# One set of five PSUM banks for scores, row maxima and turned shifts, each taking the bank whose last user is longest past

## The chip, the cores and the metric

The program runs on one core of a Trainium2 chip. The core has a matrix engine (TensorE, PE in the views), a vector engine (VectorE, DVE), an activation engine (ScalarE, ACT), GpSimd (POOL) and SyncE (SP), which issues most of the DMAs. Results of TensorE land in PSUM, which has eight banks of 128 partitions by 512 float32. The metric is the time of one execution in device microseconds (us). The kernel before took 790.63 us (median of 3 runs, 789.76 to 791.11).

## The reference

One transformer block with post-normalization, on x of shape (2, 1024, 512), 16 heads of 32 columns, feed-forward width 2048:

```python
qkv = jnp.einsum('bsd,ed->bse', x, w_qkv) + b_qkv            # split into q, k, v of 16 heads
scores = jnp.einsum('bhqd,bhkd->bhqk', q, k) / math.sqrt(Hd) # causal mask added
attn = jax.nn.softmax(scores, axis=-1)
out = jnp.einsum('bhqk,bhkd->bhqd', attn, v)
x = layernorm(x + (out @ w_out.T + b_out))
hidden = relu(jnp.einsum('bsd,hd->bsh', x, sign(up_weight)) * up_scale)
ffn = jnp.einsum('bsh,dh->bsd', hidden, sign(down_weight)) * down_scale * output_scale
x = layernorm(x + ffn)
```

## The kernel before, in words

**Stages.** The work comes in eight steps s = 0 to 7 of attention, one for each pair of a group of four heads and a batch, and behind them four blocks of 512 tokens of the feed-forward part. Every float32 operand is split into a high and a low part, and products are made of two or three matmuls.

**What a step computes.** For its four heads it needs three kinds of TensorE results that are small and short-lived:

- *Maxima* ("max", line 953): 48 matmuls per step that compute the scores of 128 queries against up to 512 keys, from which VectorE takes the largest value per query (line 786 with the causal mask, line 790 without). They are made one step ahead: in step s those of step s + 1.
- *Shifts* ("shift", line 964): two transposes per step that turn the maxima of 16 (head, tile) columns into rows. ScalarE (line 673) and VectorE (line 800) split each into a high and a low part, and two DMAs write these rows into the operand of the scores, so that the score matmul subtracts the maximum.
- *Scores* ("score", line 990): 48 matmuls per step, keys in rows and queries in columns, 128 to 512 columns wide. ScalarE takes the exponential of each (line 688) into a ring of 14 tiles, and GpSimd sets what the causal mask forbids to 0 (line 596).

Groups of four tiles then go into the weighted sum with v ("pv", line 1020, bank ps_heads) and the row sum ("sum", line 1014, bank ps_sum); twice per step VectorE normalizes 512 queries in four pairs of instructions ("norm", lines 812 and 814) and the next half's weighted sum waits for it. Between these, projections of later steps run ("proj", line 913, bank ps_proj, evicted by ScalarE in lines 661 and 667).

**What sets the order.** `plan()` gives each instruction of the whole program a slot number from tables; the sorted list `todo` is walked by every engine, and each issues its own part in that order. Each engine runs in its own order, and semaphores are the only ties. In steps 0 to 5 the first normalization of a step stands at slot 19.7 (PAIRED_NORM) and the second at 52.05, in the next step. In s = 6 the first stands at 18.4 (ALONE_NORM), ahead of the maxima 14 and 15, whose slots are 18.68 and 19.16, while the weighted sum that follows it stands at slot 24, behind scores 20 to 24. In s = 6 and 7 the output projection of the first tokens ("attn", line 1036), the sign of the late weights ("sign", ScalarE) and the split of the heads ("split") are woven in.

**The banks.** Eight banks: ps_proj, ps_unit0 to 2, ps_score0 and 1, ps_heads, ps_sum. Maximum n of a step takes ps_unit[n % 3] and waits until maximum n - 3 has been read (semaphore s_max, `unit_max_ready`). The two shifts take ps_unit0 and ps_unit2, and maxima 33 and 2 wait for their reads (s_ml, `shift_low_ready`). Score n takes ps_score[n % 2] and waits for the exponential of score n - 2 (s_exp, `probs_ready`). In the last step, when no maxima are left, scores go round four banks (ps_score0, ps_score1, ps_proj, ps_unit2). Afterwards the output projection uses ps_unit0 and 1, the first layer of the feed-forward part ("up", line 1063) ps_proj and ps_unit2, the second layer ("down", line 1080) ps_score0, ps_score1, ps_heads and ps_sum.

## Time and profile before

| | |
|---|---|
| median of 3 runs | 790.63 us (789.76 to 791.11) |
| the profiled execution | 792.56 us, its span 790.8 us |
| mean granted TensorE clock | 0.98 |
| busy share of the span | PE 94%, DVE 57%, POOL 45%, ACT 41% |
| chain of work that ended last, by engine | PE 74%, DVE 15%, ACT 3%, DMA 3%, issue 3% |
| a step of attention, s = 0 to 5 | about 50 us (88 us to 388 us) |
| s = 6 and 7 | about 388 us to 508 us |
| feed-forward part | 508 us to the end |

A view's time of an instruction is counted from the span's start. Matmuls are pipelined and their ends are modelled: a matmul of 512 columns shows 0.40 us, and the next starts well inside that. So TensorE's pace is read from start to start. A number in brackets at a row's end is idle time that the view sees before the instruction, with what ended it. The granted clock of TensorE is given as a share of 2.4 GHz: 1.00 is 2.4 GHz and 0.50 is 1.2 GHz.

### The profile page before, as it was taken

To read this page: it belongs to the slowest core of one execution; us is meant where nothing else is said; L and a number is where in the kernel's file an instruction comes from. 1 tells how busy PE (TensorE), PEld (TensorE's weight loads), DVE (VectorE), ACT (ScalarE), POOL (GpSimd) and SP (SyncE) were. 2 spreads that over 40 slices of the span, in tenths; PEclk is the share of its full clock that TensorE was granted. 3 is DMA by queue.
4 is the path that set the end of the run, shared out by engine and by line. 5 is a ranking of instruction groups with operands and counts; after the bars stand their busy time and mean duration, and the time that the engine had idled before them with its cause. 6 is when DMAs were issued, how large, how long until landed. Compare 5 with 4: busy or idle time off the path is not lost.

```text
span 790.8 us, 11678 instructions
## 1 busy us (share of the span) xinstructions
PE 745.9 (94%) x4032; PEld 502.7 (64%) x4032; DVE 451.8 (57%) x1086; ACT 323.9 (41%) x631; POOL 356.2 (45%) x487
## 2 busy tenths in 40 slices
PE   6899999999999999999999898999999999999994
PEld 4687555654656556565544453688778787878882
DVE  4176495785867858668565562533286329433514
ACT  5211365555555555456545556523232223221210
POOL 4451466384673945739332411442344234323333
PEclk9999999999999999999989899999999999999998
DMA  6966364434545256352467240503002001000101
GB/s 226 316 176 173 96 175 123 136 96 133 169 126 143 82 148 164 105 148 81 134 200 259 95 161 8 174 27 121 14 27 97 24 15 40 15 1 0 54 1 53
DMA packets 44619, 85.71 MB, mean 108 GB/s; under 512 B 4880, under 2 KB 13584, under 8 KB 44432
## 3 DMA queue, kind: packets, MB, share of 16 engines
q1 hardware_dynamic: 35536, 79.72, 33.6%
q10 hardware_dynamic: 9024, 5.24, 2.3%
q8 instruction: 32, 0.52, 0.3%
q14 instruction: 27, 0.22, 0.1%
HBM read 55.33 MB, written 29.36 MB: 107 GB/s over the span
## 4 chain that ended last, share of the span: by engine, by line
PE 74%; DVE 15%; issue 3%; ACT 3%; DMA 3%; POOL 1%; SPq 0%; ACTq 0%; DVEq 0%; POOLq 0%
PE ps_heads L1020 9%; PE ps_unit L953 8%; PE ps_score L990 7%; PE ps_proj L913 7%; PE ps_proj L1063 7%; PE ps_score L1080 6%; PE ps_unit L1036 6%; PE ps_sum L1014 5%; PE ps_unit L1063 5%; DVE maxes L790 4%; DVE heads_sb L812 4%; PE ps_heads L1080 3%; PE ps_sum L1080 3%; PE ps_sum L933 1%; PE ps_score L933 1%
## 5 line engine op out<-in xcount | busy, mean ns | idle before, releaser
L688 ACT ACTIVATE probs<-ps_score 128x512 f32<-128x512 f32 (+3 forms) x360 | 171.7, 492 | 173.7 <-PE ps_score L990 166.5
L632 POOL TENSOR_TENSOR hid_low<-hid_raw,hid_high 128x512 fp32r<-128x512 f32 x64 | 85.1, 1330 | 174.5 <-DVE hid_high L863 171.4
L786 DVE CUSTOM_DVE_ANT_0 ps_unit<-ps_unit,causal 128x128 f32<-128x128 f32 (+3 forms) x256 | 122.0, 511 | 67.9 <-PE ps_unit L953 66.4
L953 PE MATMUL ps_unit<-stack 96*128 96x512 f32 (+3 forms) x384 | 136.6, 371 | 9.9 <-DVE maxes L786 4.7
L990 PE MATMUL ps_score<-stack 98*128 98x512 f32 (+2 forms) x360 | 136.7, 386 | 4.1 <-ACT probs L688 2.3
L596 POOL TENSOR_SCALAR_AFFINE_SELECT probs<-probs 128x128 f32<-128x128 f32 x256 | 74.3, 297 | 139.5 <-ACT probs L688 134.8
L953 PEld LDWEIGHTS ps_unit<-stack 96*128 96x128 f32 x384 | 72.2, 191 | 57.7 <-DVE maxes L790 23.4
L863 DVE CAST hid_high<-hid_raw 128x512 fp32r<-128x512 f32 x64 | 27.1, 425 | 126.6 <-ACT hid_raw L743 126.3
L990 PEld LDWEIGHTS ps_score<-stack 98*128 98x128 f32 x360 | 68.4, 191 | 46.4 <-ACT probs L688 32.1
L790 DVE TENSOR_REDUCE maxes<-ps_unit 128x1 f32<-128x512 f32 x128 | 79.3, 685 | 21.3 <-PE ps_unit L953 21.2
L1020 PE MATMUL ps_heads<-probs,v_rows 128*32 128x512 f32 (+3 forms) x768 | 82.6, 508 | 5.9 <-DVE heads_sb L814 5.9
L812 DVE RECIPROCAL heads_sb<-ps_sum 128x128 f32<-128x128 f32 x64 | 60.8, 950 | 13.7 <-PE ps_sum L1014 13.7
L590 POOL TENSOR_TENSOR parts<-qk_full,parts 128x512 fp32r<-128x512 f32 x32 | 41.1, 1284 | 59.5 <-ACT parts L667 59.5
L609 POOL TENSOR_TENSOR added<-added,probs 128x512 f32<-128x512 f32 x48 | 60.9, 1284 | 0.0
L743 ACT ACTIVATE hid_raw<-ps_proj,up_scale 128x512 f32<-128x512 f32 x32 | 22.0, 689 | 93.0 <-PE ps_proj L1063 93.0
L1014 PE MATMUL ps_sum<-probs,ones 128*32 128x512 f32 (+3 forms) x576 | 58.0, 469 | 0.0
L913 PE MATMUL ps_proj<-x_high,w_high 128*128 128x512 f32 x116 | 45.9, 421 | 6.6 <-ACT x_high L645 6.6
L1080 PE MATMUL ps_score<-down_sb,hid_high 128*128 128x512 f32 x124 | 50.1, 404 | 0.0
L1080 PE MATMUL ps_score<-down_sb,hid_low 128*128 128x512 f32 x124 | 48.9, 395 | 0.0
L913 PE MATMUL ps_proj<-x_high,w_low 128*128 128x512 f32 x116 | 45.3, 412 | 0.0
L913 PE MATMUL ps_proj<-x_low,w_high 128*128 128x512 f32 x116 | 44.6, 404 | 0.0
L1020 PEld LDWEIGHTS ps_heads<-probs,v_rows 128*32 128x32 f32 x768 | 19.4, 111 | 39.6 <-issue 25.7
(185 smaller groups left out, 1224.4 us busy)
## 6 DMA issues: line engine op xcount, KB each, us to landing
stack<-qk_parts SPq DMA_DIRECT2D x96, 256.0 KB, 4.7
qk_parts<-parts SPq DMA_DIRECT2D x32, 512.0 KB, 2.9
v_all<-h_even ACTq DMA_DIRECT2D x16, 256.0 KB, 3.5
v_rows<-v_all SPq DMA_DIRECT2D x8, 512.0 KB, 4.2
heads_t<-heads_sb SPq DMA_DIRECT2D x16, 256.0 KB, 3.2
raw<-up_w SPq DMA_DIRECT2D x8, 512.0 KB, 3.6
x_tile<-x_rows SPq DMA_DIRECT2D x16, 256.0 KB, 4.7
raw<-down_w SPq DMA_DIRECT2D x8, 512.0 KB, 3.7
```

Source lines behind the costliest of these rows:

```text
L632: nc.gpsimd.tensor_tensor(hid[1][:, (HM * s + n) % 3, :], hid_raw[:, n % 2, :], hid[0][:, (HM * s + n) % 3, :].bitcast(FP32), ALU.subtract ...
L688: nc.scalar.activation(probs[:, (NP * s + n) % RING, 0:width], score_bank(s, n)[:, off:off + width], ACT.Exp, scale=SCALE).then_inc(s_exp, 1)
L786: nc.vector.tensor_tensor_reduce(ps_unit[n % 3][:, 0:width], ps_unit[n % 3][:, 0:width], causal[:, HALF - width:], 1.0, NEG, ALU.add, ALU.max,
L790: nc.vector.tensor_reduce(maxes[:, 1, col:col + 1], ps_unit[n % 3][:, :], AXIS_X, ALU.max).then_inc(s_max, 1)
L812: nc.vector.reciprocal(heads_sb[:, cols], ps_sum[:, cols]).then_inc(s_rc, 1)
L913: mm = nc.tensor.matmul(proj_bank(s, k)[:, :], ws[wp][:, c, t, :], xs[xp][:, c, t0:t0 + HALF], start=(m == 0), stop=(m == 11))
L953: nc.tensor.matmul(ps_unit[n % 3][:, 0:width], stack[s % 2][0:96, 1, f, h, i % 4 * P:(i % 4 + 1) * P], stack[s % 2][0:96, 0, c, h, 0:width ...
L990: nc.tensor.matmul(score_bank(s, n)[:, 0:width + off], stack[s % 2][0:98, 0, j // 4, h, j % 4 * P:(j % 4 + 1) * P], stack[s % 2][0:98, 1, ...
L1014: nc.tensor.matmul(ps_sum[rows, at:at + width], ones[:, :], tile, **args).then_inc(s_pv, 1)
L1020: mm = nc.tensor.matmul(ps_heads[rows, at:at + width], v_rows[:, s % 2, j, rows], tile, **args)
L1063: mm = nc.tensor.matmul(ps_up[n % 2][:, :], up_sb[n // 8][:, n % 8, m % DC, :], turned[s % 2][m // DC][:, m % DC, :], start=(m == 0), stop ...
L1080: mm = nc.tensor.matmul(ps_down[i][:, :], hid[part][:, (HM * s + n) % 3, i * P:(i + 1) * P], down_sb[:, down_at(n), :], start=(n == 0 and ...
```

## The change

A new function `share(todo)` walks the order once, before anything is issued, and hands out banks. It keeps the six banks ps_unit0 to 2 (0 to 2), ps_score0 and 1 (3 and 4) and ps_proj (5) in a list, in the order of their last use, the longest past first. Each score, maximum and shift takes the first bank of the list that it may use, and this bank goes to the list's end. Scores, maxima and shifts may use banks 0 to 4; the maxima and shifts of s = 0 only 0 to 2, since the early projections and the values of v use the score banks then; scores of the last step 2 to 5. `users` holds for each its bank and the user before it, and `had` the last user of each bank. TensorE now waits for the read of that user, whichever kind it was (`bank_read`), in place of the fixed waits. Shift 0 waits for the 16 maxima that it turns, where it waited for 31.

The end changes with it. The output projection's first matmul no longer waits for the last shift's read but for the last user of bank 0, maximum 47 of s = 7. The first two up matmuls wait for the last users of bank 5 and bank 2, score 47 and score 45 of s = 7; before, the first waited for score 46 and the second for score 47. The last users of the banks are: 0 maximum 47, 1 score 46 of s = 6, 2 score 45, 3 score 46, 4 score 44, 5 score 47.

```diff
+def share(todo):
+    order, had, users = [3, 4, 5, 0, 1, 2], {}, {}
+    for what, s, n in todo:
+        if what not in ("score", "max", "shift"):
+            continue
+        if what == "score":
+            may = (2, 3, 4, 5) if s == STEPS - 1 else (0, 1, 2, 3, 4)
+        else:
+            may = (0, 1, 2, 3, 4) if s else (0, 1, 2)
+        bank = next(k for k in order if k in may)
+        users[what, s, n] = bank, had.get(bank)
+        had[bank] = what, s, n
+        order.remove(bank)
+        order.append(bank)
+    return users, had
...
-        ps_turn = [ps_unit[0], ps_unit[2]]
...
-        def score_bank(s, n):
-            return (ps_score + [ps_proj, ps_unit[2]])[n % 4] if s == STEPS - 1 else ps_score[n % 2]
+        def bank(what, s, n):
+            return (ps_unit + ps_score + [ps_proj])[users[what, s, n][0]]
...
+            def bank_read(user):
+                if user is None:
+                    return
+                what, s, n = user
+                if what == "score":
+                    pe.wait_ge(s_exp, NP * s + n + 1)
+                if what == "max":
+                    pe.wait_ge(s_max, NU * s + n + 1)
+                if what == "shift":
+                    pe.wait_ge(s_ml, 2 * s + n + 1)
...
-                    if n == 2:
-                        wait(pe, s_ml, 2 * s)
-                    if n == NU1:
-                        pe.wait_ge(s_ml, 2 * s + 1)
-                    wait(pe, s_max, NU * s + n - 2)
+                    bank_read(users[what, s, n][1])
...
-                        pe.wait_ge(s_max, NU * s + NU1 - 2)
+                        pe.wait_ge(s_max, NU * s + NU0)
...
-                    if s == STEPS - 1 and n == 2:
+                    if s == STEPS - 1 and users[what, s, n][0] == 5:
                         pe.wait_ge(s_qk, NB * STEPS)
-                    if s == STEPS - 1 and n == 3:
-                        pe.wait_ge(s_ml, 2 * STEPS)
-                    if s < STEPS - 1 or n < 2:
-                        wait(pe, s_exp, NP * s + n - 1)
-                    elif n > 3:
-                        pe.wait_ge(s_exp, NP * s + n - 3)
+                    bank_read(users[what, s, n][1])
...
-                            pe.wait_ge(s_ml, 2 * STEPS)
                             pe.wait_ge(s_sign, 2)
                             pe.wait_ge(s_wol, 2)
+                    if s == 0 and m == 0 and i < 2:
+                        bank_read(last_user[i])
...
-                        if s == 0:
-                            pe.wait_ge(s_exp, NP * STEPS - 1)
-                    if s == 0 and n == 1:
-                        pe.wait_ge(s_exp, NP * STEPS)
+                    if s == 0 and n < 2:
+                        bank_read(last_user[(5, 2)[n]])
```

No instruction changes its place on any engine. What changes is the bank in a row and the semaphore that it waits for. The first place is TensorE in s = 3, scores 21 to 26 and maximum 16 of the next step, with projections between them. Before:

```order
L990 MATMUL ps_score1<-stack1 128x512 [waits probs_ready]
L913 MATMUL ps_proj<-x_high,w_high 128x512
L990 MATMUL ps_score0<-stack1 128x512 [waits probs_ready]
L913 MATMUL ps_proj<-x_high,w_high 128x512
L990 MATMUL ps_score1<-stack1 128x512 [waits probs_ready]
L990 MATMUL ps_score0<-stack1 128x512 [waits probs_ready]
L913 MATMUL ps_proj<-x_high,w_high 128x512
L990 MATMUL ps_score1<-stack1 128x512 [waits probs_ready]
L913 MATMUL ps_proj<-x_low,w_high 128x512
L990 MATMUL ps_score0<-stack1 128x512 [waits probs_ready]
L953 MATMUL ps_unit1<-stack0 128x512 [waits unit_max_ready,stack_filled_q1]
```

and with the change (lines 990, 953 and 913 are 1013, 981 and 945 there):

```order
L1013 MATMUL ps_unit1<-stack1 128x512 [waits unit_max_ready]
L945 MATMUL ps_proj<-x_high,w_high 128x512
L1013 MATMUL ps_unit2<-stack1 128x512 [waits unit_max_ready]
L945 MATMUL ps_proj<-x_high,w_high 128x512
L1013 MATMUL ps_unit0<-stack1 128x512 [waits probs_ready]
L1013 MATMUL ps_score0<-stack1 128x512 [waits unit_max_ready]
L945 MATMUL ps_proj<-x_high,w_high 128x512
L1013 MATMUL ps_score1<-stack1 128x512 [waits probs_ready]
L945 MATMUL ps_proj<-x_low,w_high 128x512
L1013 MATMUL ps_unit1<-stack1 128x512 [waits probs_ready]
L981 MATMUL ps_unit2<-stack0 128x512 [waits probs_ready,stack_filled_q1]
```

Nothing has moved. Scores that waited for an exponential two scores back now wait for a maximum or an exponential five users back.

The second place is TensorE in s = 6, from maximum 14 of the next step over scores 19 to 24 to the weighted sum that waits for the first normalization. Before:

```order
L953 MATMUL ps_unit2<-stack1 128x384 [waits unit_max_ready]
L990 MATMUL ps_score1<-stack0 128x512 [waits probs_ready]
L953 MATMUL ps_unit0<-stack1 128x512 [waits unit_max_ready]
L990 MATMUL ps_score0<-stack0 128x512 [waits probs_ready]
L990 MATMUL ps_score1<-stack0 128x512 [waits probs_ready]
L990 MATMUL ps_score0<-stack0 128x512 [waits probs_ready]
L990 MATMUL ps_score1<-stack0 128x512 [waits probs_ready]
L990 MATMUL ps_score0<-stack0 128x512 [waits probs_ready]
L1020 MATMUL ps_heads<-probs,v_rows 32x512 [waits probs_ready,heads_normalized]
L1020 MATMUL ps_heads<-probs,v_rows 32x512 [waits probs_ready] x3
```

and with the change (1020 is 1043 and so on):

```order
L981 MATMUL ps_unit1<-stack1 128x384 [waits probs_ready]
L1013 MATMUL ps_unit2<-stack0 128x512 [waits unit_max_ready]
L981 MATMUL ps_unit0<-stack1 128x512 [waits unit_max_ready]
L1013 MATMUL ps_score0<-stack0 128x512 [waits probs_ready]
L1013 MATMUL ps_score1<-stack0 128x512 [waits unit_max_ready]
L1013 MATMUL ps_unit1<-stack0 128x512 [waits unit_max_ready]
L1013 MATMUL ps_unit2<-stack0 128x512 [waits probs_ready]
L1013 MATMUL ps_unit0<-stack0 128x512 [waits unit_max_ready]
L1043 MATMUL ps_heads<-probs,v_rows 32x512 [waits probs_ready,heads_normalized]
L1043 MATMUL ps_heads<-probs,v_rows 32x512 [waits probs_ready] x3
```

Nothing has moved here either. Score 22 (the first with ps_unit1) now waits for the read of maximum 14, the first row, and score 24 for that of maximum 15, the third; VectorE reads both behind the normalization that the last two rows wait for.

## Rows read from the trace of the kernel before

**Rows 1.** The page, busy time of each engine over the whole span

```profile
PE 745.9 (94%) x4032; PEld 502.7 (64%) x4032; DVE 451.8 (57%) x1086; ACT 323.9 (41%) x631; POOL 356.2 (45%) x487
```

**Rows 2.** TensorE's waits, whole span: what waited, for what: us in total, times, longest

```profile
PE ps_heads L1020 <- DVE heads_sb L814: 5.9, 8, 1.4
...
PE ps_score L990 <- ACT probs L688: 2.3, 11, 0.3
...
PE ps_unit L953 <- DVE shift_l L800: 1.9, 8, 0.6
```

**Rows 3.** TensorE's timeline, s = 3: start, us, instruction, [idle before it]

```profile
255.43 0.50 PE L990 MATMUL ps_score<-stack 98*128 98x512 f32 x1
...
256.01 0.40 PE L990 MATMUL ps_score<-stack 98*128 98x512 f32 x1
256.24 0.40 PE L913 MATMUL ps_proj<-x_high,w_high 128*128 128x512 f32 x1
...
261.07 0.64 PE L1020 MATMUL ps_heads<-probs,v_rows 128*32 128x512 f32 x4
```

**Rows 4.** VectorE's timeline, the same stretch and the maxima behind it

```profile
260.21 0.29 DVE L814 TENSOR_TENSOR heads_sb<-ps_heads,heads_sb 128x128 f32<-128x128 f32 x1
...
263.46 7.87 DVE L790 TENSOR_REDUCE maxes<-ps_unit 128x1 f32<-128x512 f32 x13 [1.17 <-PE ps_unit L953]
```

**Rows 5.** TensorE's timeline, behind shift 0, in s = 3 and s = 6

```profile
273.17 0.34 PE L990 MATMUL ps_score<-stack 98*128 98x384 f32 x1
273.66 0.39 PE L953 MATMUL ps_unit<-stack 96*128 96x256 f32 x1 [0.15 <-DVE shift_l L800]
...
432.81 0.39 PE L953 MATMUL ps_unit<-stack 96*128 96x256 f32 x1 [0.63 <-DVE shift_l L800]
```

**Rows 6.** TensorE's timeline, the end of s = 3

```profile
285.01 0.51 PE L990 MATMUL ps_score<-stack 98*128 98x256 f32 x2
...
287.42 0.27 PE L964 MATMUL ps_unit<-ident,row_max 128*16 128x128 f32 x1
```

**Rows 7.** TensorE's timeline, third score of s = 0

```profile
88.61 0.50 PE L990 MATMUL ps_score<-stack 98*128 98x512 f32 x1 [0.28 <-ACT probs L688]
```

**Rows 8.** Stretches: from:to, length, each engine's busy us, clock, DMA share, GB/s

```profile
284.00:287.40 3.40, 3.02 (x12) 1.78 (x12) 2.36 (x11) 2.36 (x7) 1.45 (x5) 1.00 0.47 160
383.70:387.10 3.40, 2.70 (x10) 1.31 (x9) 2.57 (x11) 2.33 (x6) 1.45 (x5) 1.00 0.50 178
387.10:390.50 3.40, 3.40 (x35) 1.73 (x34) 0.39 (x2) 0.91 (x3) 0.59 (x2) 0.50 0.89 204
411.00:414.40 3.40, 2.27 (x12) 0.59 (x16) 2.23 (x6) 1.28 (x2) 2.36 (x1) 0.50 0.19 63
```

**Rows 9.** TensorE's timeline, weighted and row sums behind s = 5, then a score

```profile
387.45 1.08 PE L1020 MATMUL ps_heads<-probs,v_rows 128*32 128x256 f32 x8
...
390.17 0.58 PE L990 MATMUL ps_score<-stack 98*128 98x384 f32 x1
```

**Rows 10.** TensorE's timeline, first matmul of the output projection

```profile
447.99 0.77 PE L1036 MATMUL ps_unit<-w_out_high,t_even_high 128*128 128x512 f32 x1 [0.85 <-DVE shift_l L800]
```

**Rows 11.** VectorE's timeline, s = 6: maxima 14 and 15 of s = 7 are stored

```profile
412.47 0.14 DVE L786 DVE_READ_ACCUMULATOR2_ANT maxes<- 128x1 f32 x1
...
413.12 0.14 DVE L786 DVE_READ_ACCUMULATOR2_ANT maxes<- 128x1 f32 x1
```

**Rows 12.** TensorE's timeline, s = 6: scores 20 and 21, then the weighted sum

```profile
408.04 0.99 PE L990 MATMUL ps_score<-stack 98*128 98x512 f32 x2 [0.22 <-ACT probs L688]
...
412.13 1.08 PE L1020 MATMUL ps_heads<-probs,v_rows 128*32 128x512 f32 x4 [1.22 <-DVE heads_sb L814]
```

**Rows 13.** Timeline of TensorE and ScalarE, start of the feed-forward part

```profile
498.70 1.10 PE L1063 MATMUL ps_proj<-t_even_high,up_a 128*128 128x512 f32 x4
498.90 0.28 ACT L688 ACTIVATE probs<-ps_unit 128x128 f32<-128x128 f32 x1 [0.37 <-PE ps_unit L990]
...
506.79 0.50 PE L1080 MATMUL ps_heads<-down_sb,hid_high 128*128 128x512 f32 x1 [0.70 <-DVE heads_sb L814]
```

More of the change, by code:

```diff
@@ L426, in build @@
         todo = plan()
+        users, last_user = share(todo)
         block = top.enter_context(nc.Block())
@@ L672, in _ @@
                     act.wait_ge(s_mt, 2 * s + n + 1)
-                    nc.scalar.activation(shift_h[:, :], ps_turn[n][0:NU0, 0:P], ACT.Copy,
+                    nc.scalar.activation(shift_h[:, :], bank(what, s, n)[0:NU0, 0:P], ACT.Copy,
                                          scale=-1.0).then_inc(s_mh, 1)
@@ L789, in _ @@
                     else:
-                        nc.vector.tensor_reduce(maxes[:, 1, col:col + 1], ps_unit[n % 3][:, :], AXIS_X,
+                        nc.vector.tensor_reduce(maxes[:, 1, col:col + 1], bank(what, s, n)[:, :], AXIS_X,
                                                 ALU.max).then_inc(s_max, 1)
@@ L799, in _ @@
                     dve.wait_ge(s_mh, 2 * s + n + 1)
-                    nc.vector.scalar_tensor_tensor(out=shift_l[:, :], in0=ps_turn[n][0:NU0, 0:P], scalar=-1.0,
+                    nc.vector.scalar_tensor_tensor(out=shift_l[:, :], in0=bank(what, s, n)[0:NU0, 0:P], scalar=-1.0,
                                                    in1=shift_h[:, :].bitcast(FP32), op0=ALU.mult,
@@ L946, in _ @@
                         pe.wait_ge(s_stack[2 * f + 1], 48 * (s + 1))
[L947 to L953 removed]
+                    bank_read(users[what, s, n][1])
+                    nc.tensor.matmul(bank(what, s, n)[:, 0:width], stack[s % 2][0:96, 1, f, h, i % 4 * P:(i % 4 + 1) * P],
                                      stack[s % 2][0:96, 0, c, h, 0:width], start=True, stop=True).then_inc(s_unit, 1)
@@ L1043, in _ @@
                     wait(pe, s_tl, TT * s + n)
-                    if s == 0 and n == 0:
-                        pe.wait_ge(s_max, NU * STEPS)
                     for c in range(DC):
```

10 lines of the change are left out of this document (5 added, 5 removed).

## The prediction

> **What bounds the kernel now.** I read the page first: TensorE is busy for 94% of the span [rows 1]. So whatever the change brings must come from the idle 6%, and from stalls too short to be counted as idle, since matmul ends are modelled. The second view, TensorE's waits, says who holds it [rows 2]: the normalization on VectorE 5.9 us over 8 waits, the exponentials 2.3 us over 11, VectorE's read of a turned shift 1.9 us over 8. The third view is the timeline of one step of the attention part (s = 3). Six such steps, s = 0 to 5, repeat about every 50 us and look alike, s = 6 and s = 7 do not. The reader should look at the distance between the *starts* of matmuls there: back to back, a 512-column matmul takes 0.23 us from start to start (256.01 to 256.24, [rows 3]); anything longer is a stall even where the view shows no idle time. After 508 us only the feed-forward part runs, which the change does not touch.
>
> For every score, maximum and shift I compared the time at which it started with the end of the read that it waits for, by the old rule and by the new one. Two kinds of stretch come out: some in which TensorE sets the pace and stops at a short-handed bank pair (a gain), and some that end on VectorE whatever the banks do (no gain).
>
> **The change part by part.** It removes no instruction and moves none. It renames the bank of a matmul and its reader, and changes which read the matmul waits for. DMAs and queues keep their order.
>
> (a) *Scores ahead of the first normalization's end.* From 255.43 to 261.07 TensorE issues 19 matmuls, most of them 512 columns; at 0.23 us with 0.34 after a change of kind they need 4.65 us and take 5.64 [rows 3]. The 0.99 us are waits for the exponential two scores back. With five banks the user before is five back and its read is 1.5 us or more past. But the weighted sum at 261.07 also waits for the normalization, whose last instruction ends at 260.21 + 0.29 = 260.50 [rows 4]. So only 261.07 - 260.55 = 0.5 us are won per step, and the other half becomes a new wait for VectorE. Six steps: 3.1 us.
>
> (b) *The run of maxima behind it.* VectorE reads 13 of them in 7.87 us without a gap, 0.60 each [rows 4]. TensorE's stalls there are VectorE's pace. More banks let it run one matmul further ahead; the last waits stay (a maximum's bank was again used by a maximum three back). 0.1 us per step, bounds 0 and 0.5: 0.6 us. Here the Trainium skill speaks: "Perfetto Trace Analysis", section Matmul Optimizations, asks that all eight banks be leveraged for parallelism. Taken at its word this stretch would give its stalls back as well, some 0.5 us in each of six steps, and the sum would be 2 to 3 us lower; the row with 13 reads in one piece disagrees, and the row decides.
>
> (c) *Shift 0 and the maximum behind it.* In before, the maximum after the turned shift takes the shift's own bank and waits for VectorE's read: 273.17 to 273.66 is 0.49 us after a 384-column score that needs 0.18, and the restart costs another 0.1 [rows 5]. The new bank's user is a score read 2 us before. 0.42 us in each of six steps. The total of such waits is 1.9 us idle over 8 [rows 2]; six at 0.15 leave 1.0 us for two others, that of s = 6 (0.63, [rows 5]) and that of the first step (the rest, 0.37). The start of a matmul is late by some 0.2 us more than its idle time, as at 273.66, but behind the one in s = 6 the next maximum again waits for VectorE. I take 0.54 for each. 2.5 + 1.1 = 3.6 us.
>
> (d) *Scores at a step's end.* From the score that starts 0.12 after 285.01 to the shift at 287.42 there are 8 intervals, 2.29 us where 1.88 do [rows 6]: 0.41 us, and the second normalization starts that much sooner since it only waits for TensorE. Five steps give 2.05. The sixth has no projection between the scores (0.74 us by the same count). 2.8 us. The stalls after it, up to the weighted sum that waits for the second normalization, give nothing.
>
> (e) *First scores of s = 0.* No normalization is under way, so the same stalls (0.28 us idle in the first, [rows 7], then some 0.1 at every other score) are on the path: 0.9 us.
>
> (f) *The clock at 387.* The granted clock is 0.50 from 387.1 to 390.5, after a stretch in which TensorE was busy for 2.70 of 3.40 us; the same place one step sooner has 3.02 and keeps 1.00 [rows 8]. That is 1.2 GHz against 2.4. The difference is the three longer score stalls of (d). With them gone I expect the full clock: the 2.72 us from 387.45 to 390.17 [rows 9] would take half. 1.3 us, bounds 0 and 1.4.
>
> (g) *Output projection.* Its first matmul waited for the last shift's read, 0.85 us idle [rows 10]; now it waits only for the last maximum. It can start right behind the shift's turn: 0.7 us.
>
> (h) *The cost, s = 6.* Here VectorE's order puts the normalization ahead of maxima 14 and 15; their reads end at 412.47 + 0.14 = 412.61 and 413.12 + 0.14 = 413.26 [rows 11]. In before, scores 22 and 24 take the banks of scores 20 and 22 and are done while VectorE normalizes; the weighted sum starts at 412.13 [rows 12]. Now score 22 gets the bank of maximum 14 and score 24 that of maximum 15. TensorE stops after the two scores that start at 408.04 and a quarter microsecond later [rows 12], score 24 starts at 413.3 and the weighted sum at 413.55. Queued behind: scores 23 and 24, the weighted sum, then everything. Cost 1.4 us. TensorE also stands for some 4 us in one piece. It is already at 0.50 from 411.0 to 414.4 [rows 8], so I expect the same half clock, earlier or later. Bounds: 0 (if the clock is back sooner) and 3.1 (one more stretch of 3.4 us at half).
>
> (i) *The cost, first up matmul.* Its bank's last user is now the very last score, not the one before. It started at 498.70; that score's exponential ends at 498.90 + 0.28 = 499.18 [rows 13], so 0.5 us later. VectorE's copy of its result stands ahead of the last normalization in VectorE's order, and the second layer's matmul into ps_heads at 506.79 waits for that: all follow [rows 13]. 0.5 us.
>
> Sum: 3.1 + 0.6 + 3.6 + 2.8 + 0.9 + 1.3 + 0.7 = 13.0 won, 1.4 + 0.5 = 1.9 lost, 11.1 net. The profiled execution took 792.56 us (span 790.8), which gives 781.5; it was 1.9 us above the median of the runs, 790.63. On the median's scale the forecast is **779.5 us**.
>
> **Rivals.**
> 1. *The gain moves into other waits.* (a) shows the pattern: half of it already turns into a wait for the normalization. If VectorE and the exponentials catch TensorE in (c) and (d) too, each keeps half, and the clock falls at 387 as before. Then 13.0 becomes 3.1 + 0.3 + 1.8 + 1.4 + 0.5 + 0.7 = 7.8, less 1.9: 5.9 net, 784.7. For it: 57% busy VectorE, close behind in every stretch. Against: the reads that the new rule waits for ended 0.4 to 3 us sooner almost everywhere.
> 2. *More than the sum.* The half clock around 411 and the one after 445 fall on less work, or the stall in s = 6 is absorbed by the clock coming back while TensorE waits: 3 us more, 776.5.
> 3. *Slower: the clock.* In front of each normalization TensorE's idle time is gathered into one piece: from some 0.5 us (5.9 us over 8, with two long ones among them, [rows 2]) it becomes about 1, twice per step. If that were enough for the granted clock to fall as it does at 387, each fall costs 1.4 us (the 2.72 us of rows 9 halved), two in each of six steps, 16.8 us, against 11.1 won: 5.7 slower, 796.3. It decides from eight falls on. Against it: today these pieces leave the clock alone, and the fall at 387 came after several stalls in a row, not one. The Trainium skill warns of just this: "TensorE: Matmul & The Clock Gate", section "A second HAM failure mode: psum-queue depth-cycling", has a kernel whose cycling through banks leaves small idle pieces and makes the clock go to and fro. The row of 284.0 to 287.4 [rows 8], clock 1.00 with stalls in it, does not show that here so far.
> 4. *It does nothing.* If the stalls I read from starts are the pipeline's own and not waits, only (g), (h), (i) and the idle time of rows 2 count: about 1 us either way, 790. Against: stalled starts lie 0.04 to 0.06 us behind the end of a read, again and again.
>
> **How the numbers follow.** Forecast 0.64, rival 1 0.18, rival 2 0.08, rival 3 0.06, rival 4 0.04. The forecast's own terms move by a few tenths in (b), by 1.3 in (f) and by 1.7 in (h), so 776 to 783. The range for 8 in 10 takes in most of rival 1 and some of rival 2: 775.8 to 785.5. A measurement of this kernel tells 0.2% (1.6 us) from no change. Faster by more than that: forecast, rivals 1 and 2, 0.90; within it 0.04; slower 0.06.
>
> **What would show it.** TensorE's waits on exponentials and on shifts nearly gone; its waits for the normalization up from 5.9 us to 8 or more; a step from 50.0 us to about 48.5 (start of one step's second normalization to the next's). Clock 1.00 where the sixth step ends. In s = 6 a stall of some 4 us at a score, released by VectorE's maxima, then two more starts before the weighted sum. The first up matmul released by an exponential. I am wrong if the six steps keep 50 us, if the clock is below 1.00 inside them, or if scores there wait for maxima.

## The result, and the profile after

The changed kernel took **781.61 us** (median of 4 runs, 780.83 to 783.35), the kernel before 790.19 in the same comparison; the ratio is 0.9888 with a 95% interval of 0.9862 to 0.9914. Two later measurements of the same kernel gave 779.77 (ratio 0.9870, 0.9844 to 0.9896) and 780.99 us (0.9888, 0.9863 to 0.9913). The forecast was 779.5 us, with a range of 775.8 to 785.5. The profiled execution took 783.35 us, against 792.56 before: 9.2 us less, where the sum of the terms said 11.1.

The page's first line for the changed kernel, against [rows 1], and TensorE's waits over the whole span, against [rows 2] (columns as there):

```profile
PE 730.8 (94%) x4032; PEld 508.9 (65%) x4032; DVE 450.3 (58%) x1086; ACT 317.0 (41%) x631; POOL 354.9 (45%) x487
```

```profile
PE ps_heads L1043 <- DVE heads_sb L835: 10.1, 13, 1.4
...
PE ps_unit L1013 <- DVE maxes L807: 3.9, 1, 3.9
...
PE ps_score L1013 <- ACT probs L709: 1.1, 3, 0.8
```

TensorE's 4032 matmuls are the same, yet they are "busy" for 15 us less: a stall of 0.1 to 0.3 us lies inside the modelled end of the matmul before and counts as busy. The waits for exponentials have shrunk, no wait for a turned shift is left in the view, and the waits for the normalization (L1043 for L1020, L835 for L814) have grown from 5.9 us over 8 to 10.1 over 13. In s = 6 there is one new wait of 3.9 us.

Since TensorE issues the same matmuls in the same order, every one can be laid beside itself. I call *lead* how much sooner it starts in the changed kernel. Inside one like step (s = 3, starts in the kernel before):

| from | to | lead won | term, forecast |
|---|---|---|---|
| 244.23 | 255.43 | 0.28 | none |
| 255.43 | 261.07 | 0.52 | (a) 0.5 |
| 261.07 | 273.17 | -0.01 | (b) 0.1 |
| 273.17 | 275.93 | 0.44 | (c) 0.42 |
| 275.93 | 285.01 | 0.00 | none |
| 285.01 | 287.42 | 0.33 | (d) 0.41 |
| 287.42 | 294.19 | 0.00 | none |

The whole step gives 1.56 us, and its length falls from 49.96 (244.23 to 294.19) to 48.40 us. Over the program, in the profiled execution:

| stretch | lead won | forecast |
|---|---|---|
| up to 40.83, of it 1.47 in a longer half clock | -2.12 | 0 |
| first shift of the program | 0.65 | 0.54, in (c) |
| first scores of s = 0 | 1.33 | (e) 0.9 |
| steps s = 0 to 5, up to 390.17 | 10.97 | 10.3: (a) to (d), without the shifts at either end, and (f) |
| s = 6, up to 432.81 | -1.33 | -0.86: (h) and the shift of s = 6 |
| s = 7 up to the output projection | -0.51 | 0 |
| its first matmul | 0.93 | (g) 0.7 |
| then to the first up matmul | -0.67 | (i) -0.5 |
| feed-forward part | -0.03 | 0 |

The rows sum to 9.22. The second and third profile of the changed kernel (after_again and after_third below) give the same in the like steps, but not at the start and in s = 7: the row up to 40.83 is +2.40 and +1.57 there, and the one of s = 7 is -2.14 and -2.00, with the granted clock at 0.50 for 13.7 us in s = 7 where this profile has 6.8.

Term (a) is seen in TensorE's timeline of the changed kernel, s = 3, which answers to [rows 3]:

```profile
250.68 0.50 PE L1013 MATMUL ps_score<-stack 98*128 98x512 f32 x1
251.02 0.41 PE L945 MATMUL ps_proj<-x_high,w_high 128*128 128x512 f32 x1
251.27 0.40 PE L1013 MATMUL ps_unit<-stack 98*128 98x512 f32 x1
...
255.00 0.39 PE L1013 MATMUL ps_unit<-stack 98*128 98x512 f32 x1
255.81 0.64 PE L1043 MATMUL ps_heads<-probs,v_rows 128*32 128x512 f32 x4 [0.42 <-DVE heads_sb L835]
```

From the second row to the one at 255.00 the starts are 0.23 to 0.25 us apart. By the last of them 1.01 us are won, and 0.49 of these are lost again in the bracket of the weighted sum. The place behind the turned shift, against [rows 5], has no bracket any more, and 0.17 us from start to start where there were 0.49:

```profile
267.91 0.34 PE L1013 MATMUL ps_score<-stack 98*128 98x384 f32 x1
268.08 0.28 PE L981 MATMUL ps_unit<-stack 96*128 96x256 f32 x1
```

The new stall in s = 6, against [rows 11] and [rows 12]: TensorE's timeline, then VectorE's.

```profile
401.84 1.65 PE L1013 MATMUL ps_unit<-stack 98*128 98x512 f32 x3 [3.88 <-DVE maxes L807]
403.42 1.08 PE L1043 MATMUL ps_heads<-probs,v_rows 128*32 128x512 f32 x4
```

```profile
400.96 0.29 DVE L835 TENSOR_TENSOR heads_sb<-ps_heads,heads_sb 128x128 f32<-128x128 f32 x1
401.17 0.56 DVE L807 CUSTOM_DVE_ANT_0 ps_unit<-ps_unit,causal 128x384 f32<-128x384 f32 x1
401.64 0.14 DVE L807 DVE_READ_ACCUMULATOR2_ANT maxes<- 128x1 f32 x1
```

The score starts 0.06 us behind the end of the read of maximum 14 (401.64 + 0.14), and that read is queued behind the normalization, which ends at 401.25. The weighted sum could have started there; it starts at 403.42.

The clock, in stretches of the changed kernel (columns of [rows 8]): the start, the end of the sixth step, and the stall.

```profile
32.60:36.00 3.40, 1.34 (x6) 0.75 (x4) 0.00 (x0) 0.00 (x0) 1.02 (x1) 1.00 1.09 304
36.00:39.40 3.40, 2.92 (x8) 2.47 (x9) 1.45 (x5) 1.15 (x2) 0.90 (x1) 0.50 1.07 401
39.40:42.80 3.40, 3.40 (x9) 2.72 (x9) 1.55 (x5) 0.00 (x0) 1.62 (x2) 0.50 1.11 297
...
374.70:378.10 3.40, 2.87 (x17) 1.67 (x19) 2.74 (x11) 2.12 (x6) 1.29 (x5) 1.00 0.49 170
378.10:381.50 3.40, 3.40 (x42) 2.64 (x35) 2.19 (x4) 2.24 (x6) 1.29 (x5) 1.00 0.98 214
...
397.80:401.20 3.40, 0.15 (x1) 0.00 (x0) 3.30 (x7) 1.04 (x2) 0.24 (x1) 1.00 0.67 271
401.20:404.60 3.40, 2.76 (x11) 1.19 (x15) 1.23 (x5) 1.93 (x4) 0.00 (x0) 0.50 0.64 145
```

The granted clock is 1.00 at the sixth step's end, as forecast. At the start it is 0.50 for two stretches where the kernel before had one. The prediction's last sign of being wrong was a score of the like steps that waits for a maximum. The waits view, which counts idle pieces, has none. One score waits all the same, without an idle piece: in each of these steps score 35 starts 0.05 us behind the end of the read of maximum 28 (264.32 in s = 3), inside the run of maxima that VectorE paces, where no lead is won or lost.

### The profile page after: what moved, and what is told of

It is laid out like the page before. It is cut to its first block, busy times and chain, and to the rows that moved or that the text cites. A ratio compares the mean times of both kernels' runs of the same rounds, so it can differ in the third digit from the quotient of the medians.

```text
span 781.6 us, 11689 instructions
## 1 busy us (share of the span) xinstructions
PE 730.8 (94%) x4032; PEld 508.9 (65%) x4032; DVE 450.3 (58%) x1086; ACT 317.0 (41%) x631; POOL 354.9 (45%) x487
## 4 chain that ended last, share of the span: by engine, by line
PE 70%; DVE 20%; issue 3%; DMA 3%; ACT 2%; POOL 1%; SPq 0%; ACTq 0%; DVEq 0%; POOLq 0%
PE ps_heads L1043 9%; PE ps_proj L1085 7%; DVE heads_sb L833 7%; PE ps_proj L945 6%; PE ps_score L1102 6%; PE ps_unit L1061 6%; DVE maxes L811 6%; PE ps_sum L1037 6%; PE ps_unit L1085 5%; PE ps_unit L981 4%; PE ps_heads L1102 3%; PE ps_sum L1102 3%; PE ps_unit L1013 3%; DVE heads_sb L835 2%; PE ps_score L981 2%
## 5 line engine op out<-in xcount | busy, mean ns | idle before, releaser
L709 ACT ACTIVATE probs<-ps_unit 128x512 f32<-128x512 f32 (+3 forms) x215 | 101.1, 491 | 91.7 <-PE ps_unit L1013 87.9
L709 ACT ACTIVATE probs<-ps_score 128x512 f32<-128x512 f32 (+3 forms) x156 | 75.1, 496 | 76.2 <-PE ps_score L1013 73.8
L807 DVE CUSTOM_DVE_ANT_0 ps_unit<-ps_unit,causal 128x256 f32<-128x256 f32 (+3 forms) x164 | 80.4, 509 | 41.2 <-PE ps_unit L981 40.3
L981 PE MATMUL ps_unit<-stack 96*128 96x512 f32 (+3 forms) x247 | 86.0, 363 | 7.6 <-DVE maxes L807 3.8
L1043 PE MATMUL ps_heads<-probs,v_rows 128*32 128x512 f32 (+3 forms) x768 | 81.9, 504 | 10.1 <-DVE heads_sb L835 10.1
L1013 PE MATMUL ps_unit<-stack 98*128 98x512 f32 (+2 forms) x215 | 77.8, 368 | 3.9 <-DVE maxes L807 3.9
L981 PEld LDWEIGHTS ps_unit<-stack 96*128 96x128 f32 x247 | 46.7, 193 | 31.6 <-DVE maxes L811 10.9
L811 DVE TENSOR_REDUCE maxes<-ps_unit 128x1 f32<-128x512 f32 x83 | 54.3, 683 | 17.9 <-PE ps_unit L981 17.8
L1013 PE MATMUL ps_score<-stack 98*128 98x512 f32 (+2 forms) x156 | 57.2, 373 | 2.6 <-DVE h_even L789 1.5
L807 DVE CUSTOM_DVE_ANT_0 ps_score<-ps_score,causal 128x512 f32<-128x512 f32 (+3 forms) x92 | 46.1, 517 | 23.1 <-PE ps_score L981 22.8
L1013 PEld LDWEIGHTS ps_unit<-stack 98*128 98x128 f32 x215 | 41.0, 191 | 17.7 <-DVE maxes L807 4.3
L981 PE MATMUL ps_score<-stack 96*128 96x512 f32 (+3 forms) x137 | 47.7, 362 | 1.6 <-DVE maxes L807 1.1
```

The costliest lines, as they stand in the source:

```text
L709: nc.scalar.activation(probs[:, (NP * s + n) % RING, 0:width], bank(what, s, n)[:, off:off + width], ACT.Exp, scale=SCALE).then_inc(s_exp, 1)
L807: nc.vector.tensor_tensor_reduce(bank(what, s, n)[:, 0:width], bank(what, s, n)[:, 0:width], causal[:, HALF - width:], 1.0, NEG, ALU.add, ...
L811: nc.vector.tensor_reduce(maxes[:, 1, col:col + 1], bank(what, s, n)[:, :], AXIS_X, ALU.max).then_inc(s_max, 1)
L981: nc.tensor.matmul(bank(what, s, n)[:, 0:width], stack[s % 2][0:96, 1, f, h, i % 4 * P:(i % 4 + 1) * P], stack[s % 2][0:96, 0, c, h, 0:wid ...
L1013: nc.tensor.matmul(bank(what, s, n)[:, 0:width + off], stack[s % 2][0:98, 0, j // 4, h, j % 4 * P:(j % 4 + 1) * P], stack[s % 2][0:98, 1, ...
L1043: mm = nc.tensor.matmul(ps_heads[rows, at:at + width], v_rows[:, s % 2, j, rows], tile, **args)
```

## The experiments

Times are medians of 4 to 12 runs. The changed kernel stands in three comparisons with 781.6, 779.8 and 781.0 us; over its 14 runs the median is 781.1. The span times its mean granted clock takes most of the clock's part out; where it matters I give its median, as "at full clock": 765 us for the changed kernel (14 runs) and 775.4 for the one before (17 runs).

**after_again**: no edit.

> The changed kernel unaltered, as the measure for the others. In its first profiled execution the granted clock was 0.50 for 6.83 us from 36.0 us, where the kernel before had 3.41 us of it at the same place, and TensorE left that stretch 1.5 us further behind. Up to there both kernels do the same work in the same banks. Theory A (an accident of that execution, by when the first stacked tiles arrive): the stretch is 3.4 us in some executions and 6.8 in others; the first matmul behind it starts 1.5 us earlier where it is short. Theory B (something of the change): 6.83 us again. Time 781.6 us, 0.989 of the kernel before, by both.

779.77 us. The clock was 1.00 throughout the start:

```profile
32.20:35.60 3.40, 1.61 (x8) 1.07 (x7) 0.62 (x2) 0.00 (x0) 0.60 (x1) 1.00 1.08 352
35.60:39.00 3.40, 3.40 (x18) 2.83 (x17) 2.58 (x10) 1.15 (x2) 2.18 (x2) 1.00 1.07 384
```

At 40.83 the lead is +2.40 us, where the first profile had -2.12. Theory A: the half clock at the start belongs to the execution. In the profiles of the experiments below it lasts 0 or 3.4 us. At the end of the sixth step, counted from 40.83, both profiles have won the same: 12.95 us in the first, 13.06 in the second. From 40.83 to the end it is 11.34 and 10.03 us (9.60 in after_third), mainly since the half clock in s = 7 is longer in the two later ones.

**s6_apart**: term (h) undone.

```
+        if what == "score" and s == STEPS - 2 and 20 <= n <= 24:
+            may = [k for k in may if had[k][0] == "score"]
```

> Term (h) undone: in the seventh step (s = 6) scores 20 to 24 take only banks whose last user was a score, so none waits for a maximum that VectorE reads behind its normalization. Theory A (the price of the stall is what stands between the normalization's last instruction, 401.2 us in the changed kernel, and the weighted sum at 403.4): the 3.9 us wait at a score turns into a wait of the weighted sum that ends 2.1 us sooner. The new order also lets the first up matmul wait for score 44 of the last step instead of the last one, 0.65 us. Time 2.1 + 0.65 = 2.8 us below the changed kernel. Rival (the stall is absorbed by the maxima behind it, VectorE being late anyway): only the 0.65 us, or nothing. A third possibility: the half clock, 6.8 us from 401 us on, moves and falls on more or less work: 1 us either way.

777.76 us, ratio to the kernel before 0.9845 (0.9818 to 0.9871). The wait of 3.9 us at a score is gone. From the projection's matmul at 397.31 (the kernel before's time) to the weighted sum the lead changes by +0.04 us, against -2.11 in the changed kernel; at 432.81 by +0.82, against -1.33. So (h) costs 2.15 us, all of it still there 20 us later. On the way to the first up matmul the lead changes by -0.08, against -0.49 from the same place (478.50): (i) costs 0.41.

**turned_blocks**: term (c) undone.

```
+        if what == "max" and n == NU1:
+            may = [users["shift", s, 0][0]]
```

> Term (c) undone: the maximum behind the first turned shift of a step takes the shift's own bank again, all else shared as in the changed kernel. Theory A (each step's stall there was on the path): 0.42 us in each of six steps, 0.54 for the steps at either end, 3.6 us slower than the changed kernel, and TensorE's wait for VectorE's read of a turned shift back at 1.9 us over 8. Rival (the gain moves into other waits: the run of maxima behind it is VectorE's pace anyway): half of it or less, 1.8 us or under.

783.44 us. The wait is back where it was:

```profile
267.17 0.34 PE L1015 MATMUL ps_unit<-stack 98*128 98x384 f32 x1
267.67 0.39 PE L983 MATMUL ps_score<-stack 96*128 96x256 f32 x1 [0.15 <-DVE shift_l L823]
```

A like step wins 1.15 us of lead instead of 1.56, so (c) is 0.41 per step; the program's first shift wins 0.02 for 0.65, and in s = 6 the lead changes by -0.25 for +0.53 over 428.73 to 432.81, 0.78. Together 3.9 us, and at full clock 768.8 for 765. Theory A; nothing of it moved elsewhere.

**end5_pair**: scores 37 to 47 of s = 5 back on two banks.

```
+        if what == "score" and s == 5 and n >= 37:
+            may = (3, 4)
+        if what != "score" and s == 6 and (what, n) > ("max", 32):
+            may = (0, 1, 2)
```

> Term (f) tested: only at the end of the sixth step (s = 5) scores 37 to 47 keep to the two score banks and the maxima there to the other three, as in the kernel before; the rest is shared. Theory A (the half clock at 387 us in the kernel before came of these score stalls): the clock falls to 0.50 behind them again for one stretch of 3.4 us; 0.7 us of stalls and 1.3 us of clock, 2.0 us slower than the changed kernel. Rival (the half clock there was an accident of where the work fell): clock 1.00 there, 0.7 us slower. If the stalls are taken over by VectorE: 0.

779.99 us, and the lead over 360.99 to 390.17 is the same as in after_again (2.50 and 2.47 us). The experiment missed its place: the three long stalls ahead of 387 belong to the first scores of s = 6, which stand in the order before the shift that ends the step. It also changed less than it says. Three maxima stand between two scores there, so in the changed kernel too the user five back of scores 39 to 47 is the score two before; only scores 37 and 38 wait for another read in this run. What it shows is that sharing brings nothing at a step's last eleven scores.

**next_pair**: the same for those scores too.

```
+        if what == "score" and (s == 5 and n >= 37 or s == 6 and n < 4):
+            may = (3, 4)
```

> Term (f) again, at the right place. The three long score stalls ahead of the half clock at 387 us in the kernel before belong to scores 1 to 3 of the seventh step, not to the sixth step's last ones, which were tested by themselves and cost nothing. Here scores 37 to 47 of the sixth step and 0 to 3 of the seventh keep to the two score banks, the maxima there to the other three, as before the change; the rest is shared. Theory A (the half clock came of these stalls): 0.7 us or more of stalls, and the clock at 0.50 for one stretch of 3.4 us behind them, 1.3 us: 2.0 us slower than the changed kernel (781.8 by its second measurement of 779.8). Rival (the half clock was an accident of where it fell): clock 1.00 there, 0.7 us slower.

782.65 us. The stalls are back: the lead won over 360.99 to 388.75 is 1.19 us instead of 1.80, so 0.6 us. But the clock stays at 1.00. The stretches around that place, first of next_pair, then of turned_only (below), where the same stalls stand:

```profile
373.10:376.50 3.40, 2.69 (x11) 1.30 (x9) 2.56 (x11) 2.34 (x6) 1.45 (x5) 1.00 0.49 160
376.50:379.90 3.40, 3.40 (x42) 2.48 (x41) 1.80 (x4) 1.87 (x6) 0.97 (x4) 1.00 0.96 223
```

```profile
378.90:382.30 3.40, 2.70 (x10) 1.27 (x8) 2.46 (x11) 2.39 (x6) 1.45 (x5) 1.00 0.49 163
382.30:385.70 3.40, 3.40 (x36) 1.96 (x35) 0.65 (x2) 0.80 (x3) 0.58 (x2) 0.51 0.99 221
```

Busy 2.69 and 2.70 us, the same stalls one by one (starts 0.53, 0.55 and 0.64 us apart in both), and once the clock falls and once it does not. It fell there in two of the three profiles that have these stalls, and in none of the other profiles. So these stalls do not decide by themselves whether the clock falls: theory A is only half right. That the fall at this place needs them is likely (two of three profiles with them, none of the eleven others), not shown, and what decided between the two profiles above was not tested.

**turned_only**: maxima and shifts rotate over their three banks, scores keep two (four in the last step).

```
-            may = (2, 3, 4, 5) if s == STEPS - 1 else (0, 1, 2, 3, 4)
+            may = (2, 3, 4, 5) if s == STEPS - 1 else (3, 4)
-            may = (0, 1, 2, 3, 4) if s else (0, 1, 2)
+            may = (0, 1, 2)
```

> One part alone: maxima and turned shifts take the one of their three banks whose last user is longest past, scores keep to their two (four in the last step). So terms (c), (g) and (i) are there and (a), (b), (d), (e) and (h) are not. Theory A (the terms are separate and add up): the first turned shift of the program 0.56 us, 0.42 us in each of six steps, 0.8 in the seventh, 0.9 at the output projection, together 4.8 us below the kernel before, 785.6; the rest of the gain is the scores'. Rival (the terms share a wait: without the shared banks the scores' stalls take the place of the shift's): 2 us or less below the kernel before, 788.4 or more.

788.90 us, ratio 0.9979 (0.9963 to 0.9995), 12 runs. Up to 432.81 the leads add up as theory A says: 0.65 for the first shift, 0.45 in a like step, 0.78 in s = 6. But the output projection won nothing: it waits for VectorE's read of the last shift again, since that shift now is bank 0's last user. Nor is (i) there, since bank 5's last user is score 44; the expectation had (g) and (i) in this kernel. And in s = 7 the granted clock was 0.50 for 13.7 us, where the kernel before had 6.8: over 432.81 to 444.99 the lead falls by 2.3 us. At full clock it is 771.0 us, 4.4 below the kernel before; of these the runs kept 1.0. The median of their mean clocks is 0.980, that of the kernel before 0.984. The 13.7 us are not this kernel's own: the second and third profile of the changed kernel have them too. What lowers the clock in s = 7 was not tested.

**weights_later**: the first weighted sums behind each normalization a little later.

```
-PAIRED = [13, 13, 19.6, 19.6, 28, 28, 36, 36, 44, 44, 52, 52]
+PAIRED = [13.45, 13.45, 19.6, 19.6, 28.45, 28.45, 36, 36, 44, 44, 52, 52]
```

> The changed kernel, with the first weighted sums behind each normalization put one or two matmuls later in each of the six like steps (slots 13.45 and 28.45 for 13 and 28), to test why term (a) was capped. TensorE's waits for the normalization are 10.1 us over 13, some 0.8 each. Theory A (TensorE sets the pace there and this wait is the loss): each wait shrinks by 0.25 to 0.5 us, 3 to 5 us faster than the changed kernel. Theory B (VectorE sets the pace: it reads a queue of maxima without a gap after each normalization, and TensorE waits for those reads later): the waits for the normalization shrink and those for the maxima grow by as much, 0 to 1 us.

795.86 us, 15 us slower than the changed kernel; neither theory had that. At full clock it is 775.1 us, 10 above the changed kernel, so some 5 us are the clock's. The waits for the normalization fell to 2.2 us over 2. At the first place my edit put a projection's first matmul (slot 13.3) ahead of the weighted sum, and its bank is freed by ScalarE only later. TensorE's timeline and the stretches there:

```profile
242.79 0.28 PE L1013 MATMUL ps_score<-stack 98*128 98x256 f32 x1
244.59 0.50 PE L945 MATMUL ps_proj<-x_high,w_high 128*128 128x512 f32 x1 [1.52 <-ACT parts L688]
```

```profile
241.80:245.20 3.40, 1.88 (x10) 1.14 (x8) 3.33 (x10) 2.44 (x7) 2.09 (x7) 1.00 0.07 27
245.20:248.60 3.40, 3.40 (x17) 0.79 (x20) 0.79 (x3) 0.00 (x0) 0.69 (x1) 0.50 0.66 230
```

An idle piece of 1.5 us in a like step, and the clock falls to 0.50 behind it, in five of the six steps. That is the mechanism of rival 3, with a longer piece. The idle pieces ahead of the weighted sums in the changed kernel's like steps are 0.36 to 1.15 us long (12 of them, 8.7 us), and the clock is 1.00 behind each. At the second place, where only one maximum went ahead, VectorE decides: between the weighted sum that starts at 244.65 in after_again and the one behind the normalization, at 251.21 there, 1.03 us more are lost, and TensorE's waits show, once in s = 3, a maximum held up by a maximum that VectorE had not read yet:

```profile
PE ps_unit L981 <- DVE maxes L811: 1.0, 1, 1.0
```

Over the whole span the waits of maxima for such reads (L811) grow from 1.4 us over 7 to 7.1 over 13. So term (a)'s cap is real at this second place: what waits at the weighted sum would otherwise wait at a maximum. The first place says nothing of it, since ScalarE's eviction came between.

**start_filled**: eight matmuls that nobody reads, ahead of the wait at the start.

```
+                        if s == 0 and n == 0:
+                            pe.wait_ge(s_qk, NB)
+                            for _ in range(8):
+                                nc.tensor.matmul(ps_score[0][:, :], xs[0][:, 0, 0:P], wv[0][:, 0, :], start=True, stop=True)
```

> The changed kernel with eight 512-column matmuls that nobody reads, in an idle bank, where TensorE waits for the first stacked tiles (33.7 to 36.5 us in the first profile of the changed kernel). Theory A (the half clock of 0, 3.4 or 6.8 us behind that place comes of the idle time there): the granted clock stays 1.00 to the seventh step; 1.5 us less than the executions with 3.4 us of half clock, 3 less than those with 6.8, and the executions vary less among each other. On the mean 1 to 1.5 us below the changed kernel, 778.5. Rival (the half clock comes of the thin work before 30 us, or is an accident): the half clock is there as often as before, no gain.

781.68 us, no gain, with runs from 777.3 to 785.3. In the profile the half clock at the start is gone, but TensorE waited 1.7 us for a late transfer in s = 2 and the clock fell there. Inconclusive for the time.

**filled**: s6_apart with both waits filled (as above, and fourteen matmuls into ps_proj ahead of the weighted sum of s = 6).

```
+                        if s == STEPS - 2 and f == 1:
+                            pe.wait_ge(s_qk, NB * STEPS)
+                            for _ in range(14):
+                                nc.tensor.matmul(ps_proj[:, :], stack[s % 2][0:96, 1, 0, 0, 0:P], stack[s % 2][0:96, 0, 0, 0, :],
+                                                 start=True, stop=True)
```

> The seventh step mended as in s6_apart, and TensorE kept busy with matmuls that nobody reads where it stood longest: eight at the start, and fourteen of 512 columns ahead of the weighted sum that waits for the seventh step's first normalization (some 3.3 us of a wait of 3.9). Theory A (the half clock of 6.8 us from about 400 us on comes of that wait): the clock stays 1.00 there; 3.4 us below s6_apart (777.8 us), 774.4. Rival (it comes of the thin work behind the wait, in the stretch of maxima that VectorE paces, or the filled one only moves it on): the half clock is there all the same, 0 to 1 us.

778.59 us, 0.8 more than s6_apart, which is within the noise. The clock fell at 397.9, just as the fourteen began, for 3.4 us instead of 6.8; at half clock they took 4.98 us and ran past the end of the normalization:

```profile
397.73 4.98 PE L1037 MATMUL ps_proj<-stack 96*128 96x512 f32 x14
402.63 1.07 PE L1054 MATMUL ps_heads<-probs,v_rows 128*32 128x512 f32 x8
```

No long wait stood ahead of that fall. In the stretch before it TensorE was idle only for three pieces of 0.2 us, at scores that wait for an exponential:

```profile
394.40:397.80 3.40, 2.78 (x8) 1.11 (x7) 3.30 (x7) 3.20 (x8) 1.28 (x1) 1.00 0.92 357
```

So theory A does not hold as it stands: with the wait filled the clock falls all the same, for half as long. The mean clocks rose (0.986 to 0.990, against 0.980 to 0.987), and the filler cost what they gave.

**four_shared**: four banks shared instead of five.

```
-            may = (2, 3, 4, 5) if s == STEPS - 1 else (0, 1, 2, 3, 4)
+            may = (2, 3, 4, 5) if s == STEPS - 1 else (0, 1, 3, 4)
-            may = (0, 1, 2, 3, 4) if s else (0, 1, 2)
+            may = (0, 1, 3, 4) if s else (0, 1, 2)
```

> How many banks the sharing needs: scores, maxima and turned shifts of the first seven steps share four banks where the changed kernel has five; the fifth lies idle. Theory A (what counts is how far back the bank's last user lies): by the starts and reads in the second profile of the changed kernel, 18 matmuls of a step would start ahead of the read they wait for, two of them by 1.2 and 1.35 us since VectorE reads those maxima behind its normalization, as in term (h), the others by 0.2 to 0.6. Some of it is VectorE's pace already: 1 to 1.5 us in each of six steps and 2 to 4 in the seventh, 8 to 13 us slower than the changed kernel, so no faster than the kernel before (790) with its three and two. Rival (one bank fewer costs little, the rule of the longest past does it): 1 to 3 us, 782.

805.15 us, ratio 1.0193 (1.0169 to 1.0218): 24 us slower than the changed kernel and 15 slower than the kernel before. The direction is theory A's, the size twice its estimate. Its scores' waits for maxima, whole span:

```profile
PE ps_unit L1013 <- DVE maxes L807: 11.1, 10, 4.2
...
PE ps_score L1013 <- DVE maxes L807: 5.3, 6, 1.4
...
PE ps_unit L1013 <- DVE maxes L811: 2.6, 3, 0.9
PE ps_score L1013 <- DVE maxes L811: 2.5, 3, 0.8
```

21.5 us of waits of scores for maxima that VectorE reads behind a normalization or late in a run, where the changed kernel has 3.9. That is term (h) in every step.

**s6_three** and **after_third**: (h) and (i) undone by a smaller rule, beside the changed kernel.

```
+        if what == "score" and s == STEPS - 2 and 20 <= n <= 24:
+            may = [k for k in may if had[k][0] != "max" or had[k][2] < 14]
```

> Terms (h) and (i) undone by a smaller rule: in the seventh step scores 20 to 24 leave out only the banks of maxima 14 and 15, which VectorE reads behind its normalization, and rotate over three banks where s6_apart had two. Theory A: the 3.9 us wait at a score is gone, the weighted sum starts 2.1 us sooner behind the same place, the first up matmul waits for score 44; with the scores' own small stalls of s6_apart (0.2 us idle at every other one) gone too, 2 to 2.6 us below the changed kernel measured beside it. Rival (the half clock behind the wait falls on more work as the work before it is done sooner): under 1 us below it.

> The changed kernel once more, on the same chip beside s6_three, since a difference of 2 us is to be told. 780 to 782 us by its first two measurements. By theory A of s6_three the two medians lie 2 us or more apart.

779.04 and 780.99 us, 1.95 apart. TensorE's timeline of s6_three, which answers to the stall above:

```profile
396.33 0.99 PE L1015 MATMUL ps_score<-stack 98*128 98x512 f32 x2 [0.20 <-ACT probs L711]
399.24 1.93 PE L1045 MATMUL ps_heads<-probs,v_rows 128*32 128x512 f32 x8 [1.91 <-DVE heads_sb L837]
```

s6_three gives (g) up, though: bank 0's last user is the last shift again, and the lead changes by -0.79 at the output projection, where s6_apart has +1.17. Both versions with (h) undone are faster than the kernel before, and by their medians than the changed kernel. That second difference is not clear of the noise in the times (the intervals of the ratios overlap); it rests on the leads. Their 10 runs have a median of 778.4 us, the 14 of the changed kernel 781.1. The half clock of 6.8 us behind the stall stays in both, so it does not come of the wait at the score.

## Why the prediction was right, and where it was off

- **(a)** Right to 0.02 us per step, with its cap: 1.01 us won, 0.49 given to the wait for the normalization. weights_later shows at its second place that VectorE sets this cap.
- **(b)** 0.1 forecast, none found.
- **(c)** 0.42 forecast; 0.44 by the leads, 0.41 by turned_blocks. The program's first shift was worth 0.65, that of s = 6 0.53 to 0.78, forecast 0.54 each.
- **(d)** 0.41 forecast, 0.33 found: 0.08 us stay behind the step's first score, whose bank VectorE frees; what holds them there was not tested. Some 0.28 us per step between 244.23 and 255.43 were in no term: I counted one stretch ahead of the first normalization and left out the scores behind the weighted sums at 244.23.
- **(e)** 0.9 forecast, 1.33 found. I had taken the 0.1 us that the matmul *behind* a stalled score is late for a cost of changing kind. TensorE's timeline of the kernel before, then of the changed one, at the same place:

```profile
89.79 0.44 PE L990 MATMUL ps_score<-stack 98*128 98x384 f32 x1
90.08 0.39 PE L913 MATMUL ps_proj<-x_low,w_high 128*128 128x512 f32 x1
```

```profile
90.58 0.34 PE L1013 MATMUL ps_score<-stack 98*128 98x384 f32 x1
90.76 0.40 PE L945 MATMUL ps_proj<-x_low,w_high 128*128 128x512 f32 x1
```

  The same pair is 0.29 us apart behind a stall and 0.18 without one. A stall costs its own length and 0.1 more. A change of kind costs nothing: the rows of term (a) above change kind at 0.23 to 0.25 us.
- **(f)** 1.3 forecast, 1.28 found in the two profiles compared. As a property of the kernel it is less: with the same stalls the clock fell in two profiles of three.
- **(g)** 0.7 forecast, 0.93 found. It hangs on which user comes last at bank 0; in turned_only it was nothing.
- **(h)** -1.4 forecast, -2.1 found. The stall was the one foretold, 3.88 us, released by the read of maximum 14. What failed is the term's size. I had score 24 start as soon as maximum 15 is read and the weighted sum a quarter microsecond behind it, 0.9 us behind score 22. But the clock is at 0.50 from 401.23 on: score 24 starts at 402.86, 0.4 us behind that read, the weighted sum 0.56 later, and from score 22 it is 1.58 us. I had written of the half clock there, and had it in the bounds but not in the sum.
- **(i)** -0.5 forecast, -0.49 found.
- **The sum.** The two us by which the first profiled execution falls short are none of the terms: from 40.83 us on the lead grows by 11.34 us, against 11.1 forecast. Before that place 2.12 us were lost, 1.47 of them to a second stretch of half clock that another execution of the same kernel does not have. That 11.34 and 11.1 agree so well is in part luck. (e), (g) and the 0.28 us per step that no term had (1.7 us in six) make up for (b), (d), (h) and 0.5 us lost in s = 7. In the two later profiles the same growth is 10.03 and 9.60 us, mainly for the longer half clock in s = 7, which I had not priced. By the medians the change brought 8.6, 10.6 and 8.9 us.
- **Rival 1** (gain into other waits) holds only where (a) said so. **Rival 2** did not come: the half clock in s = 6 lasts 6.8 us in both kernels. **Rival 4** (stalls that are no waits) is out, since a like step gained 1.56 us. **Rival 3** (clock) did not come: the granted clock is 1.00 in all of s = 1 to 5. The Trainium skill, "TensorE: Matmul & The Clock Gate", section "A second HAM failure mode: psum-queue depth-cycling", describes a kernel whose small idle pieces do make the clock go to and fro; the changed kernel's pieces of 0.36 to 1.15 us did not. weights_later brought a fall about with pieces of 1.5 us, at five of six places. The other rule of the Trainium skill that I weighed, all eight banks in use ("Perfetto Trace Analysis", "Matmul Optimizations"), would have had a gain in (b), and there was none: VectorE's pace, not a short bank, sets the time there. four_shared, which leaves one bank idle, was 24 us slower than the changed kernel, which agrees with the rule. At full clock the change is worth 10.4 us (775.4 less 765).

## What to carry to other kernels

Compare, for each use of a buffer, the start of the writer with the end of the read it waits for, and ask which engine makes that read and what is queued ahead of it there: against the kernel before, five shared banks gained 9 us and four lost 15. When buffers are shared between readers, keep a short-lived result off a buffer whose read stands behind a long instruction of the other reader (2 us here, for two lines). Lay each matmul beside itself in the two traces before naming a cause: the lead shows in one table which stretch won and which part was only the clock.

## What the runs showed of the hardware

The granted clock differs between executions of one kernel. In three profiles of the changed kernel the half clock behind the start lasted 6.8, 0 and 0 us, and its runs had mean clocks from 0.978 to 0.986 and times from 777.9 to 783.4 us. A difference below 2 us between two kernels needs the leads, or several runs side by side. The half clock in s = 7 lasted 6.8, 13.7 and 13.7 us in the same three profiles. A matmul that follows one that waited starts 0.1 us late (0.29 us against 0.18 behind 384 columns, 0.34 against 0.23 behind most that have 512).
